# Weighting and sums of a tile of keys issued together in odd slots, in three attentions of a decoder kernel

## What is computed

```python
scores = jnp.einsum('bhqd,bhkd->bhqk', q, k) * scale
attn = jnp.einsum('bhqk,bhkd->bhqd', jax.nn.softmax(scores, axis=-1), v)
```

## Time and profile before

| | us |
|---|---|
| median of 3 runs | 3032.38 |
| lowest and highest | 3022.53, 3037.97 |
| span of the profiled execution | 3028.2 |
| median less that span | 4.2 |
| TensorE busy in the span | 2476.7 (82%) |
| VectorE, ScalarE, GpSimd busy | 1884.0, 1239.5, 851.9 |
| mean granted clock of TensorE | 0.900 |

### The profile page before, as it was taken

One profiled execution on the slowest core, in us unless ns is written; L12 is line 12 of the kernel. 1 busy time (PEld: TensorE's weight loads), 2 busy tenths in 40 slices (PEclk: granted clock), 3 DMA queues, 4 the chain that ended last, 5 costly groups with the idle time before them and its releaser, 6 DMA issues. The chain is left out here.

```text
span 3028.2 us, 35090 instructions
## 1 busy us (share of the span) xinstructions
PE 2476.7 (82%) x12822; PEld 1644.7 (54%) x12822; DVE 1884.0 (62%) x2959; ACT 1239.5 (41%) x1873; POOL 851.9 (28%) x1176
## 2 busy tenths in 40 slices
PE   5898989864443357999448999999999879999999
PEld 4454545321222237998334554545555538888887
DVE  3766575627899985778557777565655444444443
ACT  2444444428656625666103433334333323333332
POOL 2232222215657634555343332001211110000000
PEclk8999999976665678999768999999999979999999
DMA  3213132212222346988585655334433423101000
GB/s 117 65 43 84 43 84 46 70 61 77 77 80 77 108 163 213 308 300 289 158 185 136 159 146 157 88 89 104 109 95 91 115 80 127 42 0 42 1 28 15
DMA packets 186940, 323.55 MB, mean 107 GB/s; under 512 B 20450, under 2 KB 52066, under 8 KB 186788
## 3 DMA queue, kind: packets, MB, share of 16 engines
q1 hardware_dynamic: 168356, 270.44, 30.0%
q0 software_dynamic: 15360, 50.34, 6.3%
q10 hardware_dynamic: 3072, 0.79, 0.1%
HBM read 182.30 MB, written 62.92 MB: 81 GB/s over the span
## 5 line engine op out<-in xcount | busy, mean ns | idle before, releaser
L757 DVE TENSOR_REDUCE at_negmax<-at_ps 128x2 f32<-128x1024 f32 (+3 forms) x256 | 259.1, 1016 | 120.3 <-PE at_ps L523 63.1
L670 ACT ACTIVATE at_probs<-at_ps 128x1024 f32<-128x1024 f32 (+3 forms) x256 | 221.7, 866 | 267.4 <-PE at_ps L538 263.3
L1367 DVE TENSOR_REDUCE a_negmax<-a_ps 128x2 f32<-128x1024 f32 x128 | 155.2, 1217 | 136.4 <-PE a_ps L1120 135.8
L59 PE MATMUL ff_ps<-ff_xnT_hi,ff_s_hi 128*128 128x512 f32 x512 | 200.8, 392 | 5.1 <-DVE ff_xnT_lo L2878 5.1
L60 PE MATMUL ff_ps<-ff_xnT_lo,ff_s_hi 128*128 128x512 f32 x512 | 200.1, 391 | 0.0
L61 PE MATMUL ff_ps<-ff_xnT_hi,ff_s_lo 128*128 128x512 f32 x512 | 200.1, 391 | 0.0
L1946 ACT ACTIVATE gr_act_signs<-gr_signed,gr_test 128x512 bf16<-128x512 f32 x248 | 177.4, 717 | 42.3 <-POOL gr_test L2339 20.4
L2908 DVE TENSOR_TENSOR ff_hid<-ff_hid,ff_ps 128x512 f32<-128x512 f32 x64 | 44.0, 688 | 238.6 <-ACT ff_hid L2853 238.6
L538 PE MATMUL at_ps<-at_qk 98*128 98x512 f32 (+3 forms) x512 | 171.7, 417 | 21.0 <-DMA at_qk<-at_mrow 10.6
L1268 ACT ACTIVATE a_probs<-a_ps 128x1024 f32<-128x1024 f32 x128 | 130.8, 1023 | 135.2 <-PE a_ps L1138 134.6
L518 PE MATMUL at_ps<-at_qk 96*128 96x512 f32 (+3 forms) x512 | 162.9, 382 | 19.0 <-DVE at_xnT_lo L818 8.9
(11 more groups left out here) (431 smaller groups left out, 6640.1 us busy)
## 6 DMA issues: line engine op xcount, KB each, us to landing
at_qk<-at_part SPq DMA_DIRECT2D x384, 128.0 KB
first_gu<-in_L_ffn_w_gate_up_dram SPq DMA_DIRECT2D x32, 1024.0 KB, 13.4
a_qk<-a_part SPq DMA_DIRECT2D x192, 128.0 KB
first_d<-in_L_ffn_w_down_dram SPq DMA_DIRECT2D x32, 512.0 KB, 13.6
out_rows<-ex_y SPq DMA_DIRECT2D x32, 512.0 KB
gr_aside_raw<-in_L_ffn_W_dram SPq DMA_DIRECT2D x48, 256.0 KB, 3.1
w13T<-gr_aside_out SPq DMA_DIRECT2D x32, 256.0 KB, 3.2
shared_x<-x_after_cross SPq DMA_DIRECT2D x8, 1024.0 KB
```

Source lines behind the costliest of these rows:

```text
L59: pe.matmul(out, lh, rh, start=start, stop=False, skip_group_check=True)
L670: act.activation(probs[:, t % 2, 2 * w:2 * w + 2, lo:S], banks(("kq", g, s), lo), ACT.Exp, scale=SCALE).then_inc(free(("kq", g, s)), 1)
L757: dve.reduce_max(negmax[:, g % 2, :].rearrange("p (j t) -> p j t", t=NT)[:, 2 * w:2 * w + 2, t], banks(("qk", g, s), 0, width(g, t)), AX.X ...
L1367: dve.reduce_max(negmax[:, g % 2, :].rearrange("p (j t) -> p j t", t=NT)[:, 2 * w:2 * w + 2, t], banks(("qk", g, s)), AX.X, negate=True).t ...
```

## The change

In odd slots from slot 3 TensorE issues the weighting and the sums of one tile one behind the other, and nothing in even slots; the last tile's two come in slot 1 of the next group. ScalarE's copies of NUM and SUMS move from slots 0 and 1 to 1 and 2, and the reciprocals from slots 2 to 5 to slots 3 to 6 (not those of the linear block's even groups). `half` goes. The same is done in both functions; the diff shows the second wherever it differs.

```diff
@@ attention_layers @@
         def reciprocal_part(s):
-            return s - 2 if 2 <= s < 2 + NT else None
+            return s - 3 if 3 <= s < 3 + NT else None
...
-            def half(g, n):
-                if n % 2 == 0:
-                    weigh(g, n // 2)
-                else:
-                    add_up(g, n // 2)
-
...
-                    if s >= 2 and has(g):
-                        half(g, s - 2)
-                    if s < 2 and has(g - 1):
-                        half(g - 1, PAIRS - 2 + s)
+                    if s % 2 and s >= 3 and has(g):
+                        weigh(g, s // 2 - 1)
+                        add_up(g, s // 2 - 1)
+                    if s == 1 and has(g - 1):
+                        weigh(g - 1, NT - 1)
+                        add_up(g - 1, NT - 1)
...
-                    if s == 0 and has(g - 1):
+                    if s == 1 and has(g - 1):
                         act.wait_ge(values_done, NT * g)
...
-                    if s == 1 and has(g - 1):
+                    if s == 2 and has(g - 1):
                         act.wait_ge(sums_done, NT * g)
...
@@ attention_linear @@
             if g % 2:
-                return (s - 2,) if 2 <= s < 2 + NT else ()
+                return (s - 3,) if 3 <= s < 3 + NT else ()
             if g % NC == 0:
                 return (s - 4,) if s >= 4 and s < PAIRS else ()
...
```

More of the change, by code:

```diff
@@ L1160, in add_up @@
                 mm.then_inc(sums_done, 1)
[L1162 to L1166, removed]
             def turn_features(m):
```

## The result

The changed kernel takes **3099.5 us** (median of 4 runs, 3095.8 to 3102.1) against 3032.4 for the kernel before: a ratio of 1.022, with a 95% interval of [1.020, 1.024]. The forecast was 3064 with a range up to 3094, so the sign was right, the size was half of what came, and the range did not hold it.

The account below looks back on a forecast made before the run. TensorE was taken to set the pace. Terms 7.4 + 3.3 + 1.2 + 7.1 - 2.1 + 7.7 + 10 - 2.5 = 32 us on the 3028.2 us profile gave 3060, plus 4.2 for the median: 3064 us, range 3018 to 3094.

Parts of the forecast that it names:

- The merger's saving: Both blocks: fewer changes between full-column and column-group matmuls save 0.32 us per merged pair; unstalled plain pair 3.96 us.
- The stall that takes it back: Plain pair of slots: odd query scores wait for ScalarE's exponential, a 0.43 us stall; pair 4.39 us against 4.28.
- Slots 0 and 1: Layers, group start: key scores wait for projection's banks; 4.63 us against 4.14, plus 0.49 in 15 groups; causal plus 0.22.
- The pair behind the values: Layers, slots 4 and 5: exponential waits for the values' copy; 4.73 us against 4.17, plus 0.56 in 8 groups.
- Slots 2 and 3 of the odd linear groups: TensorE waits longer for ScalarE's copy of turned features: plus 1.8 us in three groups, 0.8 in four, 8.6 in all.
- Rival 1: Both blocks: drains count and the stall does not appear, so faster: 2971 us, or 3000 if half; chance 0.12.
- rival 2: No change: plain pairs as worked out, edge waits partly taken up by existing waits; plus 8, 3040 us; chance 0.25.
- Linear block, odd groups ... 10 us: Longer wait for the features' copy in slots 2 and 3, plus 0.25 us at later pairs in three groups; 10 us.
- Rival 4: Much slower: longer gaps also lower TensorE's granted clock by 0.03 over both blocks, 30 to 45 us more, 3100; chance 0.13.
- End of a group: Layers, slots 6 and 7: fourth reciprocal delays the last maximum, plus 0.86 us in 7 groups; all ends together 7.7 us.
- The causal pairs, slots 4 and 5: Layers, plain causal groups: shorter exponentials leave the full saving, minus 0.24 us per pair.
- Outputs behind the even slot: Layers, slots 4 and 5: an output projection covers the exponential, minus 0.3 us in 7 groups, 2.1 us.

Follow-up runs that it names:

- x6: Changed kernel, but in slots 3 and 5 the weighting and sums stand between the key scores and the query scores; 3127.3 us.
- x4: Changed kernel plus 16 transposes of the identity behind slot 2's transpose of features in the linear block's odd groups, output unchanged; 3077.8 us.
- x5: Changed kernel, but in the linear block's odd groups the first tile's weighting and sums go to slot 2, behind the transpose of features; 3077.1 us.
- x3: Changed kernel, but in the two layers the four reciprocals go to slots 3, 3, 4, 5 instead of 3, 4, 5, 6; 3064.8 us.

## Why the forecast was right in sign and wrong in size

**Right.** The merger's saving (weighting to sums 0.88; 4.02 for the pair without a stall in x6, bound 3.96). The stall that takes it back (4.36, forecast 4.39). Slots 0 and 1 at 4.56 to 4.57 (forecast 4.63) and plus 0.22 in causal groups. The pair behind the values at 4.70 (forecast 4.73). Slots 2 and 3 of the odd linear groups, once the clock is held, in sum only (8.2 us, forecast 8.6). Rival 1, the drains alone, is refuted by the wait of 0.18 at the odd query scores of the full plain pairs, rival 2 by both blocks.

**Wrong, first: the step "Linear block, odd groups ... 10 us".** It priced the wait as its length. The block grew by 29 us, x4 takes 21.6 of them back with work added, x5 takes 22.4 back with work moved. Rival 4 held this mechanism with a chance of 0.13, and the argument against it, "the gaps are under 1 us nearly everywhere", contradicted the forecast's own 1.9 us ("some 1.9 us of waiting") in seven groups. Its size was guessed as a mean over both blocks; it sits behind single gaps of 2.0 to 2.3 us. Its mean fall of 0.03 came in the linear block only; the layers' clock fell by 0.01. That its 3100 us is the time that came is partly luck: some 21 us of clock are shown in the linear block, 6 behind four projections and most of 2.7 in the layers' second group, and 7 more us are longer ends of groups, which it did not have.

**Wrong, second: the step "End of a group".** The reciprocal's 0.86 was right, but it was moved alone. Its reader, the multiplication on GpSimd, moved with it onto the added rows (2.33 instead of 1.53), so 1.65 came instead of 0.86; and the projection behind ran at half clock in four places. The term counted seven groups; six have it, since the first has no group before it whose sums could be inverted, so 9.8 us came where 6.0 were forecast. For the seven groups that turn the next x in slot 6 the forecast had a range from minus 1.00 to plus 0.86 each and took minus 2.4 us for all; plus 1.7 came. With added rows two of them lost 1.8 and 2.9 (9.10 to 10.85, 7.86 to 10.79), without them the others gained 0.5 to 0.9 (one from 7.83 to 6.96). Which of the contention and the half clock makes how much of the 2.9 was not measured apart; x3 removes two thirds of it (8.85), and the granted clock over these two slots is 0.84 in after, still 0.85 in x3, and 1.00 before. Ends and projections were forecast at 7.7 us and came at 21.9; x3 makes them minus 11.2.

**Wrong, third, and small.** The causal pairs, slots 4 and 5: minus 0.14 (3.48 to 3.34) instead of minus 0.24. Outputs behind the even slot: minus 0.20 to 0.28 instead of 0.3. The 2.7 us in slots 4 and 5 of the layers' second group are the clock again: from the odd key scores to the next even ones TensorE took 5.57 us at a granted clock of 0.51, for work of about 3.0 us at full clock (a plain pair's 1907.96 to 1911.29 us less its stall of 0.35), behind waits of 2.12 and 1.75 us for VectorE's maxima. In the kernel before the waits there were 2.00 and 1.54, and the clock stayed at 1.00; why it fell behind the one pair and not behind the other is open.

## What to carry to other kernels

Price a wait on TensorE not by its length alone: with matmuls all around, an idle time of about 2 us can cost its length and then several microseconds at half clock. It did not each time (2.33 us twice and 2.00 once left the clock as it was), so it is a risk with a price. First look whether a regrouping makes one gap out of two small ones. When an operation is moved, move with it in the forecast whoever waits for it, on every engine, and look at what runs there at the same time. Merging work saves the change-over, but the piece that lay between was also the cover of another engine's latency: merge only where something else covers it.

## What the runs showed of the hardware that was not expected

- An idle time of 2.12 us of TensorE, in a stretch at a granted clock of 1.00, is followed by 8 us at a mean of 0.57; 16 transposes in the gap keep 1.00 and make the kernel 21.6 us faster. Waits of 0.92 in the kernel before did not do this in the same place: the granted clock stayed at 1.00 over the 8 us from 350 us.
- The length of one idle time does not settle it: three waits of 1.84 to 1.86 us in the odd linear groups (ahead of the query scores at 151.85, 308.79 and 465.75 us) and two of 2.33 in the layers (ahead of the transposes at 1726.29 and 1862.89 us) left the clock at 1.00, and one of 1.88 in the kernel before (1658.37 us) was followed by 4 us at 0.57.
- VectorE's two scalar-tensor-tensor operations took 2.33 us beside a GpSimd multiplication and 1.53 without, the multiplication 1.61 and 1.29, alike behind eight groups.
- The clock's share of a change need not lie where the change is: a reciprocal of 0.94 us on VectorE decides whether TensorE's matmuls of the next projection take 0.40 or 0.63.
